# Graph edges sorted by source and destination block before they are counted, in a fused GPS layer on one core

## The reference, cut to what matters

```
edge_index = stack([src, dst]);  xn = layernorm(x)
# graph part: loops are added once more, deg counts a node's incoming edges
src, dst = concat([src, loop]), concat([dst, loop])
deg = segment_sum(1, dst);  norm = rsqrt(deg)[src] * rsqrt(deg)[dst]
gnn = segment_sum((xn @ W)[src] * norm, dst) + b
# linear attention over all nodes
q, k, v = split(xn @ W_qkv);  q1, k1 = softmax_kernel_features(q), (k)   # k: one maximum over everything
mix = (q1 @ (k1^T v)) / (q1 @ sum(k1)) @ W_proj + b_proj
x = x + gnn + mix
# mixture of experts: expert 0 for every token, and 3 routed ones
x = x + sum_e combine[:, e] * (layernorm(gelu(xn2 @ fc1[e] + b1[e])) @ fc2[e] + b2[e])
```

## Time and profile before

| | |
|---|---|
| median of 3 runs | 1272.68 us (1272.11 to 1272.81) |
| the profiled execution | 1272.19 us |
| span of its instructions | 1270.5 us |
| busy: PE, PEld | 1223.6 us (96%), 1088.4 us (86%) |
| busy: DVE, ACT, POOL | 813.5 us (64%), 702.2 us (55%), 282.5 us (22%) |
| mean granted clock of TensorE | 0.99 |
| first fc1 matmul | at 483.05 us |

### The profile page before, as it was taken

One profiled execution on the slowest core, in us unless ns is written; L12 is line 12 of the kernel. 1 busy time (PEld: TensorE's weight loads), 2 busy tenths in 40 slices (PEclk: granted clock), 3 DMA queues, 4 the chain that ended last, 5 costly groups with the idle time before them and its releaser, 6 DMA issues.

```text
span 1270.5 us, 21747 instructions
## 1 busy us (share of the span) xinstructions
PE 1223.6 (96%) x7068; PEld 1088.4 (86%) x7069; DVE 813.5 (64%) x1367; ACT 702.2 (55%) x1098; POOL 282.5 (22%) x184
## 2 busy tenths in 40 slices
PE   5899999999999999999999999999999999999985
PEld 5899999997688857888889998888999888899975
DVE  8567676416446774762585686465596598655983
ACT  3412233427526431543686768566677796676863
POOL 1000000003120010026253243231343271323421
PEclk8899999999999999999999999999999999999998
DMA  9100000000014312312669656647657887386943
GB/s 324 50 1 1 1 1 1 1 1 26 2 27 164 118 56 73 112 25 45 221 257 330 223 207 245 198 151 277 215 210 276 310 320 228 129 311 214 355 149 95
DMA packets 55394, 188.97 MB, mean 149 GB/s; under 512 B 7626, under 2 KB 8260, under 8 KB 55346
## 3 DMA queue, kind: packets, MB, share of 16 engines
q1 hardware_dynamic: 47858, 170.07, 35.8%
q0 software_dynamic: 6448, 17.91, 6.9%
q10 hardware_dynamic: 1040, 0.33, 0.1%
HBM read 176.70 MB, written 14.51 MB: 151 GB/s over the span
## 4 chain that ended last, share of the span: by engine, by line
PE 85%; DVE 5%; issue 3%; ACT 3%; DMA 2%; POOL 0%; ACTq 0%; DVEq 0%; POOLq 0%; SPq 0%
PE bank L1815 23%; PE bank L1799 22%; PE bank L1527 8%; PE bank L1598 5%; PE bank L1616 4%; PE bank L1736 3%; PE bank L1638 3%; PE bank L1651 3%; PE bank L1783 2%; PE bank L1693 2%; PE bank L1671 2%; PE bank L1787 2%; DMA out<-ysb,sidx 2%; PE bank L1776 1%; PE bank L1682 1%
## 5 line engine op out<-in xcount | busy, mean ns | idle before, releaser
L492 ACT ACTIVATE w2hi<-w2raw 128x1536 fp32r<-128x1536 f32 x96 | 139.6, 1485 | 89.0 <-DMA w2raw<-in_L_ffn_fc_w 80.9
L505 DVE TENSOR_TENSOR w2lo<-w2raw,w2hi 128x1536 fp32r<-128x1536 f32 x96 | 164.2, 1752 | 22.3 <-ACT w2hi L492 19.9
L747 POOL DMA_INDIRECT out<-ysb,sidx x27 | 122.9, 4552 | 235.4 <-issue 203.6
L1815 PE MATMUL bank<-w2hi,hthi 128*128 128x384 f32 x624 | 161.5, 339 | 0.0
L1815 PE MATMUL bank<-w2lo,hthi 128*128 128x384 f32 x624 | 159.0, 335 | 0.0
L1815 PE MATMUL bank<-w2hi,htlo 128*128 128x384 f32 x624 | 158.8, 335 | 0.0
L492 ACT ACTIVATE w1hi<-w1raw 128x1536 fp32r<-128x1536 f32 x96 | 137.8, 1500 | 30.9 <-DMA w1raw<-in_L_ffn_fc_w 30.2
L505 DVE TENSOR_TENSOR w1lo<-w1raw,w1hi 128x1536 fp32r<-128x1536 f32 x80 | 143.4, 1858 | 3.6 <-ACT w1hi L492 3.6
L1527 PE MATMUL bank<-ohd,ohs 125*125 125x313 bf16 x825 | 130.3, 306 | 16.0 <-DVE ohd L847 14.8
L1799 PE MATMUL bank<-w1hi,xthi 128*128 128x512 f32 x486 | 139.7, 396 | 3.9 <-POOL w1lo L505 3.9
L1799 PE MATMUL bank<-w1lo,xthi 128*128 128x512 f32 x486 | 136.8, 390 | 0.0
(11 more groups left out here) (305 smaller groups left out, 1982.6 us busy)
## 6 DMA issues: line engine op xcount, KB each, us to landing
w1raw<-in_L_ffn_fc_w SPq DMA_DIRECT2D x96, 768.0 KB, 6.5
w2raw<-in_L_ffn_fc_w SPq DMA_DIRECT2D x96, 768.0 KB, 6.6
wg<-in_L_gnn_W SPq DMA_DIRECT2D x1, 2304.0 KB, 13.4
wv<-in_L_mix_W_qkv SPq DMA_DIRECT2D x1, 2304.0 KB, 19.8
wk<-in_L_mix_W_qkv SPq DMA_DIRECT2D x1, 2304.0 KB, 24.3
wq<-in_L_mix_W_qkv SPq DMA_DIRECT2D x1, 2304.0 KB, 24.1
out<-xs SPq DMA_DIRECT2D x5, 375.0 KB
xn_dram<-xn SPq DMA_DIRECT2D x5, 375.0 KB
```

What stands on the lines that cost most here:

```text
L492: act.activation(unit(w2hi if second else w1hi, second, u), unit(w2raw if second else w1raw, second, u), ACT.Copy).then_inc(w2_hi if secon ...
L505: eng.tensor_tensor(unit(w2lo if second else w1lo, second, u), unit(w2raw if second else w1raw, second, u), unit(w2hi if second else w1hi, ...
L747: pool.indirect_dma_start(out=out, out_offset=bass.IndirectOffsetOnAxis(ap=sidx[:, 0:1], axis=0), in_=ysb[:, :], in_offset=None, bounds_ch ...
L1815: last = pe.matmul(y_ps[s][:, 0:384], a[:, c, :], w[:, c, 384 * s:384 * s + 384], start=c == 0 and k == 0, stop=False)
```

## The change

The edges are sorted first. Each edge belongs to one of 25 buckets (source block x destination block). On DVE, 25 comparisons give a one-hot `ehot` over buckets, a running sum `erun` of it (in two halves) each edge's rank within its partition, and two small PE products (`bucket_ranks`) the ranks over partitions. Every bucket starts at a new tile of 128 places; `edge_slots` works out each edge's place, and **165 indirect scatters on POOL**, at most 8 in flight, write each edge's pair (source and destination within their blocks) into a table in HBM that was filled with -1. The table has 185 tiles of 128 places. It is read back by SP once all scatters have landed, DVE makes one-hots of 125 columns for each tile (ring of 48), and PE does **one product of 125 columns per tile**, into a column region of PSUM that it reads from a register (`where`). The registers are loaded 16 at a time. The order changes: the key features come ahead of q; the counting stands beside the output projection; degrees and messages come behind it. Weights q are loaded later, `xs` a second time.

The diff, cut to its core (`...` marks what is left out):

```
+ET_TILES = (EDGES + BUCKETS * 127) // 128
+RING = 48
+IN_FLIGHT = 8
+ONES_AT, MAX_AT = 16, 76
@@ SP
+            load_qkv("v", 2 * D)
+            load_qkv("k", D)
+            sp.wait_ge(epad_ok, 1)
+            sp.dma_start(edge_dram.rearrange("(p w) a -> p w a", p=128), epad[:, :, :].bitcast(I32)).then_inc(st_epad, 16)
...
+            done(sp, ("xt", "l", 4))
+            sp.wait_ge(eslot_ok, 1)
+            load_qkv("q", 0)
...
             done(sp, ("kv", H - 1))
-            sp.dma_start(wpb[:, :, :], w_proj.rearrange("(c p) n -> p c n", c=C)[:, 4:6, :]).then_inc(ld_wp, 16)
             for u in range(C):
                 load(False, 0, u)
...
+            edges_stored(sp)
+            sp.dma_start(etab[:, :, :].bitcast(I32), edge_dram.rearrange("(p w) a -> p w a", p=128)).then_inc(ld_edges, 16)
...
+            done(sp, ("pj", NT - 1, 1))
+            sp.dma_start(gatew[:, 0:C * E].rearrange("p (c n) -> p c n", c=C),
+                         gate_w.rearrange("(c p) n -> p c n", c=C)).then_inc(ld_gate, 16)
@@ POOL
+            pool.wait_ge(eslot_ok, 1)
+            pool.wait_ge(st_epad, 16)
+            for k in range(ET):
+                if k == ONES_AT:
+                    done(pool, ("h", NT - 1, 1))
+                    pool.memset(vext[:, :, :, HD:HD + 1], 1.0).then_inc(vones_ok, 1)
+                if k == MAX_AT:
+                    pool.wait_ge(kmax_ok, 1)
+                    pool.partition_all_reduce(kmax[0:TP, 1:2], kmax[0:TP, 0:1], TP, RMAX).then_inc(kall_ok, 1)
+                if k >= IN_FLIGHT:
+                    pool.wait_ge(st_edges[k % IN_FLIGHT], 16 * (k // IN_FLIGHT))
+                pool.indirect_dma_start(out=edge_dram, out_offset=bass.IndirectOffsetOnAxis(ap=eslot[:, k:k + 1], axis=0),
+                                        in_=epair[:, k, :].bitcast(I32), in_offset=None).then_inc(st_edges[k % IN_FLIGHT], 16)
...
+            edges_stored(pool)
+            pool.memset(bsplit[:, :], 0.0).then_inc(bsplit_zero, 1)
...
+            for i in range(NT):
+                pool.wait_ge(ld_x[i], 64)
                 pool.tensor_tensor(xs[:, i, :], xs[:, i, :], bias2[:, 0, :], ALU.add).then_inc(x_biased, 1)
@@ DVE
+            link(run(0, BUCKETS // 2))
             for n, (kind, k) in enumerate(T8):
                 x_lower(kind, k)
             split_low(dve, "h", 0)
+            link(run(BUCKETS // 2, BUCKETS))
+            bucket_totals()
             split_low(dve, "h", 1)
+            edge_slots()
             split_low(dve, "v", 0)
+            tile_regions()
+            split_biases()
             split_low(dve, "v", 1)
             split_low(dve, "k", 0)
             split_low(dve, "k", 1)
...
+            split_low(dve, "q", 1)
+            square("q", 0)
+            squares_to(("sqk", 0), 0)
             dve.wait_ge(kall_ok, 1)
...
+                    if i == NT - 1 and p in (0, 1):
+                        dve.wait_ge(ld_edges, 16)
+                        one_hots(9 * p, 9 * p + 9)
...
+            one_hots(18, RING)
+            for n in range(7):
+                upto = min(ET_TILES, RING + (ET_TILES - RING) * (n + 1) // 7 + 3)
+                one_hots(done_tiles, upto)
+                done_tiles = upto
+                if n < 6:
+                    add_projection(n // 2, n % 2)
@@ PE, behind the transposes "at"
+            for n in range(COUNT_BANKS):
+                pe.matmul(bank[n][0:TP, 0:width], eye[:, 4 * TP:5 * TP], eye[:, a:a + width], start=True, stop=False,
+                          skip_group_check=True)
...
+            def count(a, b):
+                for t in range(a, b):
+                    if t % OFFSETS == 0:
+                        where[:] = nc.values_load_multi_w_load_instructions(
+                            offs[0:1, t:min(t + OFFSETS, ET_TILES)], engines=[mybir.EngineType.PE], min_val=0, max_val=REGION[-1],
+                            skip_runtime_bounds_check_because="the table holds a region's column, and regions are capped at the last")[1]
+                    pe.wait_ge(oh_ready, t + 1)
+                    last = pe.matmul(banks[0:TP, bass.ds(where[t % OFFSETS], TP)], ohs[:, t % RING, 0:TP], ohd[:, t % RING, 0:TP],
+                                     start=False, stop=t == ET_TILES - 1, skip_group_check=True)
+                    last.then_inc(oh_free, 1)
+            def project_out(n):
...
+                    m = C * n + c
+                    if m < TILES_BESIDE:
+                        count(ET_TILES * m // TILES_BESIDE, ET_TILES * (m + 1) // TILES_BESIDE)
+            for n in range(2 * NT - 2):
+                project_out(n)
+            pe.wait_ge(adj_ok, COUNT_BANKS)
...
+            project_out(2 * NT - 2)
+            project_out(2 * NT - 1)
+            pe.wait_ge(h_scaled, NT)
+            pe.wait_ge(ld_gate, 16)
...
-            project_out(0)
-            project_out(1)
-            project_out(2)
+            messages(0)
+            messages(1)
+            messages(2)
             turn_xn2(0)
             gate(0)
```

More of the change, by code:

```diff
@@ L66 @@
 END_TURN_AT = 6
[L69 to L94, removed]
 class Chain:
@@ L345, in gps_kernel @@
         groups([("at",) + k for k in T8], R8)
+        for n in range(2 * NT):
+            groups([("pj", n // 2, n % 2)], [0 if n == 2 * NT - 2 else 7])
+            if n == 2 * NT - 3:
+                groups([("deg", 0)], [1])
         def two(name, i, banks):
@@ new lines, in _, with run @@
+            link(dve.scalar_tensor_tensor(out=ebucket[:, :], in0=eq[:, 0, :], scalar=float(NT), in1=eq[:, 1, :],
+                                          op0=ALU.mult, op1=ALU.add))
+            for b in range(BUCKETS):
+                last = dve.tensor_scalar(ehot[:, b, :], ebucket[:, :], float(b), None, ALU.is_equal)
+            link(last)
+            def run(a, b):
+                hot = ehot[:, a:b, :].rearrange("p b k -> p (b k)")
+                return dve.tensor_tensor_scan(erun[:, a:b, :].rearrange("p b k -> p (b k)"),
+                                              ones[0:TP, 0:1].broadcast_to([TP, (b - a) * ET]), hot,
+                                              0.0 if a == 0 else erun[:, a - 1, ET - 1:ET], ALU.mult, ALU.add)
@@ L1054, in x1_and_norm @@
+            split_lo(dve, False, 0, range(2))
+            add_projection(4, 0)
+            add_projection(4, 1)
+            for s in range(2):
+                for i in range(NT):
+                    taken(dve, ("pj", i, s))
+            split_lo(dve, False, 0, range(2, C))
             def x1_and_norm(i):
                 for s in range(2):
-                    ps = read(dve, ("pj", i, s))
+                    ps = read(dve, ("gnn", i, s))
                     part = xs[:, i, 384 * s:384 * s + 384]
-                    last = dve.tensor_tensor(part, ps[0:TP, 0:384], part, ALU.add)
@@ L1445, in _ @@
             x_high(1)
-            done(act, ("pj", NT - 1, 1))
-            for i in range(2):
+            done(act, ("gnn", NT - 1, 1))
+            for i in range(NT - 1):
                 act.wait_ge(st_xn2[i], 16)
@@ new lines, in _ @@
+            for n in range(2 * NT - 2):
+                project_out(n)
+            pe.wait_ge(adj_ok, COUNT_BANKS)
+            ps = fill(pe, ("deg", 0))
+            for o in range(NT):
+                for b in range(NT):
+                    last = pe.matmul(ps[0:TP, WIDE * o:WIDE * o + WIDE], adj[:, TP * (NT * b + o):TP * (NT * b + o) + TP], ones[0:TP, :],
+                                     start=b == 0, stop=b == NT - 1)
+            filled(last, ("deg", 0))
+            project_out(2 * NT - 2)
```

659 lines of the change are left out of this document (340 added, 319 removed).

## The result

The changed kernel takes **1266.1 us** (median of 5 runs, 1265.83 to 1266.61) against 1272.68 of before: 0.9949, 95% interval 0.9935 to 0.9964. It is faster by 0.5%, and inside the range, but the gain is 6.6 us where the prediction (1241) had 31.7.

The account below looks back on a forecast made before the run. PE was taken to bound the kernel. Of 105 us of counting products removed some 31 arrive, 31 go to new counts, the rest to the table wait and degrees: fc1 at 453.0 against 483.0, total 1241 us, range 1206 to 1288.

Parts of the forecast that it names:

- h started: Start of the kernel: first h matmul at 33 (bounds 31 and 38), before about 37.5.
- the 77th scatter: POOL takes the key maximum only behind 76 scatters, at about 179; PE stalls in q from 167 to 180.
- the next item: One-hots ahead of the last tile: 4.7 us, POOL's hold 5.5, attention results 1.7; last tile done at 336.
- the 1.4 us that the last message pair was to save: Behind the first fc1: the last message pair saves 1.4 us, the expert loop unchanged.
- The sort's places: DVE's edge places ready at 60, with 6.0 us of passes and 4.4 of reduction; 65 if strided reading doubles it.
- 165 scatters, POOL: Scatters 245 us, DVE's delays 15, memset and maximum 1.5, ending at 321.5; table load 2.5, in at 324.
- table to last count: After the table: last tile at 336, transposes 5.4, unit products 1.6, seven projection groups 27.4, counting 31; DVE hidden behind PE.
- 9.4 us for that case: Counting stage: 185 counts if product cost scales by columns (125 of 313); 23.5 us was taken instead.
- Last count to fc1: One group 3.9, bank copies 0.5, degrees 6.0, two groups 7.8, gate weights 2.5, messages 30.9; fc1 at 453.0.
- Scatters in time: Rival, chance 0.30: undelayed scatters and earlier places, PE's chain ends last; fc1 at 436, total 1224, or about 1203.
- DVE holding POOL whole: Rival, chance 0.14: DVE passes hold POOL's scatters for 43 us instead of 15; table at 352, total 1269.
- The sequencer: Rival, chance 0.18: PE's register loads in the counting stage, 56 us if all exposed; total 1290.

Follow-up runs that it names:

- max_early: Changed kernel with the key maximum taken behind 57 scatters instead of 76; 1265.93 us, 0.9952 of before.
- max_on_pe: Changed kernel with POOL's maximum over partitions replaced by one PE product and a DVE reduction; 1256.27 us, 0.9870 of before.
- beside4: best4 with the counts spread beside projection groups 2 to 7 instead of behind all of them; 1237.38 us, 0.9714 of before.
- best4: spread4 plus max_on_pe's edit, the bucket sum by planes, and 48 tiles of one-hots between the last projection additions; 1241.67 us, 0.9778 of before.
- projection_first: Changed kernel with 16-tile one-hots, table wait behind eight projection groups, all counts after them, maximum behind 57 scatters, bias additions reordered; 1247.45 us, 0.9803 of before.
- batched: Changed kernel with one-hots of 16 tiles made in one DVE operation, tile innermost, so PE reads with a stride; 1282.35 us, 1.0083 of before.
- beside1: beside4 with each tile's one-hots laid together, so PE reads without a stride; 1255.69 us, 0.9875 of before.
- spread4: projection_first with one-hots of 4 tiles interleaved instead of 16, 8 bytes between columns instead of 32; 1253.17 us, 0.9839 of before.
- half_scatters: Changed kernel without 80 of the 165 scatters, so most edges are missing from the counts; 1249.88 us, 0.9831 of before.

## Why the prediction was half right

**Held.** h started at 33.1 (33); the chain does run places, scatters, table, last tile; DVE waited for a DMA of the table ahead of its first one-hot; PE stalled in q behind the 77th scatter (the maximum came at 194.6, not near 179), and by the prediction this "costs nothing beyond the next item": max_early shows that. The loop is unchanged (787.4 and 787.4), so the 1.4 us that the last message pair was to save behind fc1 did not come.

**Wrong, the table: in at 342.5, not 324.** The steps that failed are "The sort's places" and "165 scatters, POOL", whose sum gives the table; item by item:
- Places at 66.2, not 60: 25 passes took 7.6 (6.0), the strided reduction 7.9 (4.4; the prediction named the doubling and did not take it), and the first scatter starts 1.0 behind DVE's last step.
- The maximum over partitions cost POOL 5.96 + 0.38, where the sum had under 1.5. Before, the same gap may have lain under a true wait, of 5.83 us for DVE's maximum. But 7.58 us without a releaser were to be seen there ahead of POOL's next IOTA:

```profile
309.17 0.38 POOL L678 PARTITION_ALL_REDUCE kmax<-kmax  x1 [5.83 <-DVE kmax L952]
...
345.92 0.16 POOL L682 IOTA biota_i<- 128x36 int32 x1 [7.58 <-issue]
```

The Trainium skill, "GPSIMD Engine Reference", Instruction dispatch, states that the first call to a freshly loaded kernel pays about 6 us with no instruction to be seen. The trace agrees in size (5.96), and shows more than it says: 7.2 ahead of the first addition behind it. max_on_pe, in which both gaps are gone, ties them to this instruction.
- DVE's passes held the scatters for 19.8 us (216.1 less 165 x 1.19), not 15.
- A scatter takes 1.49 with its issue, not 1.484 (1.1 in 165), and the table is in 3.9 behind the last one, not 2.5: SP's load leaves 1.6 behind its end and takes 2.3 to land.

6.2 + 5.1 + 4.8 + 1.1 + 1.4 = 18.6, measured 18.5.

**Right for the wrong reason, table to last count:** 78.2 us, predicted 77.4. The prediction had PE as the bound ("DVE needs ... 47 from 336, PE 65: hidden"). It is the other way round: a count costs PE 0.06 to 0.07, not 0.127 and registers, and DVE's one-hots start every 0.163, not 0.13, 60.5 in all, and 9.7 of hold (taken 5.5, "0 to 11"). The two errors cancel, which is luck: with the right price of a count alone, 12 us for 185, the same sum would have given 58. The price of a product was taken from one whose columns were 2.5 times as many, though the working had 9.4 us for that case; the one-hot's from an operation with a third of the columns. The Trainium skill, "SBUF — State Buffer", Who interferes with whom, has DVE in a two-port mode and GpSimd shutting each other out for the whole instruction, and names tensor_scalar, the form of the one-hots, among those that can enter such a mode. For DVE's one-hots behind POOL's additions the trace agrees: 1.73 to 1.77 for six of the starts, the length of one addition (1.78).

**Last count to fc1:** 56.8, predicted 51.6 (3.9 + 0.5 + 6.0 + 7.8 + 2.5 + 30.9). The copies of the banks leave PE waiting 2.4, not 0.5, and the group behind it takes 5.8, not 3.9: after a wait PE's records are slower for a while, as above (1.64 for two at 377.27, 0.86 for two before the stall). From the first message to fc1 it is 33.0, not 30.9; the degrees were 0.6 shorter.

18.5 + 0.8 + 5.2 = 24.5 us: fc1 at 477.6, not 453.0.

**The rivals.** Scatters in time: no. DVE holding POOL whole: 19.8 us of the 43, so in part, and in the other direction too. The sequencer: by the bulk form 16 registers come in one instruction of 0.86 to 1.30 us, 12 of them, so the 56 us were 13 at most. Hidden here and in beside4, 10 us in best4, where the cover is gone.

## What to carry to other kernels

When work moves from one engine to a chain of others, add up each of the others alone, from the moment its input is there: here DVE's 370 one-hots were longer than everything PE had left. Batching such operations made them cheap here (0.07 each, not 0.163), but the result must be laid out for its reader, since PE's speed fell with the bytes between its columns. What batching is worth in all is not measured: no run has projection_first's order with single one-hots. And count what an engine does between two kinds of instruction: a single GpSimd maximum over partitions cost 6 us ahead of it and 7 ahead of the next addition, and one PE product with two small DVE operations replaced it.

## What the runs showed of the hardware

- A 128x125 bf16 product with its weight load takes 0.06 to 0.07 us beside fp32 products with columns next to each other, 0.11 if they start 8 bytes apart; the mean weight load is 0.145, 0.204 and, at 32 bytes, 0.321 us (changed kernel, beside4, batched).
- A DVE comparison of two f16 tensors with 2000 results takes 1.19 us if both run in order innermost (beside4), 2.23 if one stands still (beside1).
- The granted clock of PE fell in the key-value and query stages with PE over 90% busy: in spread4 to 0.67 to 0.83 from 230 to 290, in beside4 to 0.50 from 240 to 260. In projection_first, which issues the same products as spread4 there, it was 0.98 on the mean, and the stretch 20 us shorter. It differs between executions of one kernel too.
- GpSimd and DVE hold each other both ways: a 2-element DVE operation took 1.30 us beside GpSimd's addition, 0.16 elsewhere (half_scatters); a scatter that started at 103.08, 1.0 us into a DVE subtraction of 2.56, took 2.63 instead of 1.19 and ended 1.1 behind it (changed kernel).
